# Row sums of the softmax in the first local attention: from a VectorE reduction to two mask columns in the product with V

## The chip, the cores and the metric

The kernel is one launch on one core of a Trainium2 chip. The metric is the device time of that core in microseconds (us), the median over several executions. The core's engines run their own instruction streams and meet only at semaphores: TensorE (PE; its weight loads are listed apart as PEld), VectorE (DVE), ScalarE (ACT), GpSimd (POOL), and SyncE (SP) for transfers. All of this kernel's matmuls are float32, and each one shows as two records in the trace.

## The reference

The program is a small language model tower of two layers over 64 x 256 tokens with 64 channels: embedding with a layer norm, a recurrent attention, a mixture of 8 experts, then windowed attention, then a graph attention that gates 4 experts. The change concerns the windowed attention alone ("first local attention", `L1_attn`):

```python
def _L1_attn_ref(x, qkv_w, qkv_b, proj_w, proj_b):
    H, W = (8, 64); HD = C // H                       # 8 heads of 8 channels, windows of 64 tokens
    qkv = (xw @ qkv_w + qkv_b).reshape(Bv, nW, W, 3, H, HD)
    q, k, v = (qkv[..., 0, :, :], qkv[..., 1, :, :], qkv[..., 2, :, :])
    attn = jnp.einsum('bwihd,bwjhd->bwhij', q, k) * HD ** (-0.5)
    attn = jax.nn.softmax(attn, axis=-1)
    out = jnp.einsum('bwhij,bwjhd->bwihd', attn, v).reshape(Bv, nW, W, Cv)
    return out @ proj_w + proj_b
...
h = h + _L1_attn_ref(_layernorm(h, axis=-1), ...)
```

There are 16384 tokens, so 256 windows of 64.

## The kernel before, in words

The 16384 tokens are 128 tiles of 128 rows (two windows of 64 tokens each). The attention takes four tiles at a time: four "lanes" (`AL`), each with its own two PSUM banks (`ps[0]` for small things, `ps[1]` for the 128 x 512 scores) and its own buffers, in a loop of `AI` = 32 iterations. The order is written out by hand. Each engine runs through a list of steps (`A_STEPS`), and each step is issued for lane 0, 1, 2, 3 before the next step begins (`step`). A step waits by `need` for the counters of the steps it depends on, and adds one to its lane's counter of its own engine.

The steps of one iteration, with the engine: `xs` (ACT, copy of the normalised tile), `xT` (PE, turn it), `xTs` (ACT), `qkv` (PE), `q` (ACT, two 64 x 64 copies, L817), `kb` (DVE, keys times the head mask, 128 x 512, L1193), `vb` (DVE, values times a two-column mask `vmask`, L1196), `sc` (PE, scores of 8 heads, 128 x 512), `mx` (DVE, row maxima, L1198), `sb` (DVE, scores less maxima into `B.E`, L1199), `ex` (ACT, exp of `B.E`, L819), `sm` (DVE, row sums of `B.E`, 128 x 512 to 128 x 8, L1200), `PT` (PE, turn the exponentials), `PTs` (ACT, copy to SBUF, L820), `rc` (DVE, reciprocal of the 8 sums, L1201), `pv` (PE, product with V: 8 matmuls per lane with 64 x 16 outputs, a pair of heads each), `on` (DVE, that product times the reciprocals, L1202), `oT` (PE, turn the result), `oTs` (ACT, L821), `pj` (PE, output projection), `h` (DVE, add to the residual, L1205).

The values in `B.V` are laid out by window and pair of heads. Of 128 rows (turned: a pair of heads by 64 keys), head 0 of the pair uses the first 64 and head 1 the last 64; `vmask` has a one in its column 0 for the former and in its column 1 for the latter. `xT` of the next iteration waits for `h` of its lane, so iterations hardly overlap. In some iterations VectorE also does a piece of an unrelated index preparation (`prepare`), in front of `kb`. Ahead of the loop VectorE makes the masks and clears or fills parts of the lanes' buffers (L1136 to L1143); the first `xT` of a lane waits for that. Every matmul is recorded at the helper line L389, so PE groups are told apart by their shapes.

Of the kernel before, what the change touches and what calls it, by code (L numbers as in the profile page):

```python
# [19 lines left out]
ACT_STEPS="h0s xs V th za sgt tw ta sq e1 e2 e3 lnk rn BKs Ats gts bons p2s p4s p8s EEs MKVs E2s Z0s W1Ts S1 S2 S3 Os osq lnv rstd yTs".split()  # L20
DVE_STEPS="oneh sg w cs cm a kq ssm kn A R b0 B t1 kp K rk g1 g2 l o d1 d2 d4 d8 Z1 W U1 U2 U3 mu oc var on gw gb bv ob og h".split()
COLS="b_w b_a k_k k_a r_k mr mw mk mv ma mg b_w2 b_a2 nk_a".split()
A_STEPS=dict(pe="xT qkv sc PT pv oT pj".split(), act="xs xTs q ex PTs oTs".split(), dve="kb vb mx sb sm rc on h".split())
G_STEPS=dict(pe="xT hg".split(), act="xs xTs hgs".split(), dve="ms rs md rd".split())
Y_STEPS=dict(pe=["h0","h1","y0","h2","y1","h3","y2","y3"], act=[f"g{e}" for e in range(4)], dve=["b0","b1"])
NE=262144; EC=NE//P
# [28 lines left out]
def prog(nc, x, embT_d, w1T_d, tb1_d, w2T_d, rows_d, proj_d, wv_d, ag_d, lora_d, bg_d, wo_d, cols_d,  # L55
         gam_d, wr_d, br_d, w1_d, b1_d, w2_d, b2_d, qkv_d, proj1_d, wg_d, att_d, lw1_d, lb1_d, lw2_d, lb2_d, fin_d, edges, out):
    with ExitStack() as ctx:
        sb=lambda n,s,d=F32: ctx.enter_context(nc.sbuf_tensor(n,s,d))
# [66 lines left out]
        for l in range(LANES):  # L125
            B=Lane(PS[4*l:4*l+4],sem(f"pe_step_{l}"),sem(f"act_step_{l}"),sem(f"dve_step_{l}"),1); L.append(B)
# [34 lines left out]
        iot=sb("iota8",[P,8]); iot_i=sb("iota8_i",[P,8],I32); mk_i=sb("mask_iota",[P,2],I32); mkf=sb("mask_iota_f",[P,2])  # L161
# [9 lines left out]
        take=bump(C0+8192,D0)  # L171
# [4 lines left out]
        for l in range(2):  # L176
            B=Lane(PS[4*l:4*l+4],None,None,None,0); FL.append(B)
# [4 lines left out]
        s_gw=sem("ffn0_gates"); s_wt=sem("ffn0_gates_turned"); s_ws=sem("ffn0_gates_copied"); s_fc=sem("ffn0_constants"); s_gs=sem("gate_rows_stored"); NK=NT//8  # L182
        AL=lanes("attn1",4,2,first=1); take=bump(C0+8192,D0)
        for B in AL:
            B.xs=take([D]); B.xT=take([P]); B.Q=take([P]); B.K=take([8,D]); B.V=take([2,D]); B.E=take([8,D])
            B.PT=take([4,P]); B.mx=take([8]); B.rs=take([8]); B.o=take([D]); B.oT=take([P])
        GL=lanes("gat",2,4,first=1); take=bump(C0+8192,D0)
        for B in GL:
# [199 lines left out]
        def _(pe):  # L388
            mm=lambda o,a,b,st=True,sp_=True: nc.tensor.matmul(o,a,b,start=st,stop=sp_,skip_group_check=True)  # L389
# [5 lines left out]
            for v in range(2):  # L395
                r=mm(ps0[1][:,v*D:(v+1)*D],hT[:,v*P:(v+1)*P],w2T[:,:])
# [242 lines left out]
            with pe.Fori(0,AI) as i:  # L639
                def step(fn,*names):  # L640
                    for B in AL:
                        need(pe,B,A_STEPS,i,*names)
                        fn(B).then_inc(B.pe,1)
                def xT(B):
                    pe.wait_ge(B.dve,i*len(A_STEPS["dve"])+1)
                    return mm(B.ps[0][0:D,0:P],B.xs,ident[:,:])
                step(xT,"act:xs")
                def qkv(B):
                    for h,s in HALVES:
                        w=slice(h*D,(h+1)*D)  # L650
                        mm(B.ps[0][s,P:P+D],aw[0:D+1,0:D],B.xT[0:D+1,w])
                        mm(B.ps[0][s,P+D:2*P],aw[0:D+1,D:2*D],B.xT[0:D+1,w])

                        for _,s2 in HALVES: r=mm(B.ps[0][s2,2*P+h*D:2*P+(h+1)*D],B.xT[0:D+1,w],aw[0:D+1,2*D:3*D])
                    return r
                step(qkv,"act:xTs")
                step(lambda B: mm(B.ps[1][:,:],B.Q,B.K.rearrange("p h j -> p (h j)")),"act:q","dve:kb")
                def PT(B):
                    for g in range(4): r=mm(B.ps[1][:,g*P:(g+1)*P],B.E[:,2*g:2*g+2,:].rearrange("p a b -> p (a b)"),ident[:,:])
                    return r  # L660
                step(PT,"act:ex","dve:sb")
                def pv(B):
                    for h,s in HALVES:
                        for g in range(4):
                            r=mm(B.ps[0][s,384+g*16:384+(g+1)*16],B.PT[:,g,h*D:(h+1)*D],B.V[:,h,g*16:(g+1)*16])
                    return r
                step(pv,"act:PTs","dve:vb")
                step(lambda B: mm(B.ps[0][0:D,0:P],B.o,ident[:,:]),"dve:on")
                step(lambda B: mm(B.ps[0][:,448:512],B.oT[0:D+1],ap[0:D+1]),"act:oTs")
            ended(pe,AL,A_STEPS,AI)  # L670

            with pe.Fori(0,GI) as i:
# [37 lines left out]
        def _(act):  # L710
# [162 lines left out]
        def _(dve):  # L873
            V=nc.vector; n=[0]
            def lk(ins):
                n[0]+=1; ins.then_inc(s_v,1); dve.wait_ge(s_v,n[0])
# [260 lines left out]
            lk(V.tensor_scalar(mk_i[:,0:1],mk_i[:,0:1],6,None,ALU.logical_shift_right))  # L1137
            lk(V.tensor_copy(mkf[:,:],mk_i[:,:]))
            V.tensor_scalar(hmask,iot[:,:],mkf[:,1:2],None,ALU.is_equal)
            V.tensor_scalar(vmask,iot[:,0:2],mkf[:,0:1],None,ALU.is_equal)  # L1140
            for B in AL:
                V.memset(B.xT[D:D+1],1.0); V.memset(B.oT[D:D+1],1.0)
                V.memset(B.Q[0:D,D:P],0.0); V.memset(B.Q[D:P,0:D],0.0).then_inc(B.dve,1)  # L1143
            for B in AL: dve.wait_ge(B.dve,1)
            dve.wait_ge(s_w2,16*8)
            h8=lambda t: t.unsqueeze(2).broadcast_to((P,8,D))
            sc=lambda B: B.ps[1][:,:].rearrange("p (h j) -> p h j",h=8)
# [39 lines left out]
            for i in range(AI):  # L1187
                prepare(i)
                def step(fn,*names):
                    for l,B in enumerate(AL):  # L1190
                        need(dve,B,A_STEPS,i,*names)
                        fn(B,l).then_inc(B.dve,1)
                step(lambda B,l:V.tensor_tensor(B.K,B.ps[0][:,P+D:2*P].unsqueeze(1).broadcast_to((P,8,D)),h8(hmask),ALU.mult),"act:q")  # L1193
                def vb(B,l):
                    v=lambda t: t.rearrange("p (g e d) -> p g e d",g=8,e=2)
                    return V.tensor_tensor(v(B.V.rearrange("p w f -> p (w f)")),v(B.ps[0][:,2*P:3*P]),vmask.unsqueeze(1).unsqueeze(3).broadcast_to((P,8,2,8)),ALU.mult)  # L1196
                step(vb,"pe:qkv")
                step(lambda B,l:V.tensor_reduce(B.mx,sc(B),AX.X,ALU.max),"pe:sc")  # L1198
                step(lambda B,l:V.tensor_tensor(B.E,sc(B),h8(B.mx),ALU.subtract),"dve:mx")  # L1199
                step(lambda B,l:V.tensor_reduce(B.rs,B.E,AX.X,ALU.add),"act:ex")  # L1200
                step(lambda B,l:V.reciprocal(B.rs,B.rs),"dve:sm")  # L1201
                step(lambda B,l:V.tensor_tensor(B.o.rearrange("p (h d) -> p h d",h=8),B.ps[0][:,384:448].rearrange("p (h d) -> p h d",h=8),B.rs.unsqueeze(2).broadcast_to((P,8,8)),ALU.mult),"pe:pv","dve:rc")  # L1202
                def hh(B,l):
                    v=H[:,bass.ds(i*4+l,1),:]
                    return V.tensor_tensor(v,v,B.ps[0][:,448:512].unsqueeze(1),ALU.add)  # L1205
                step(hh,"pe:pj")
            ended(dve,AL,A_STEPS,AI)
            norm(2)
# [87 lines left out]
            for g in range(NG):  # L1296
# [47 lines left out]
                for u in range(N//8):  # L1344
# [6 lines left out]
                    v=H[:,k*8:k*8+8,:]  # L1351
# [37 lines left out]
```

## Time and profile before

| | |
|---|---|
| median of 3 executions | 6361.67 us (6355.64 to 6379.33) |
| the profiled execution's own time | 6358.16 us |
| its span, first to last instruction | 6356.4 us |
| this attention in it (first `kb` to last `h`) | 2171 to 2757 us, 586 us |
| in that stretch: PE busy, DVE busy, ACT busy | 500.92, 423.27, 283.52 us |
| mean granted TensorE clock, whole span / this stretch | 0.653 / 0.94 |

Busy time is time in which an engine has an instruction under way; overlapping matmul records are counted once. In the timeline, "x4" means four instructions merged into one row, whose duration is from the first's start to the last's end; the bracket is the engine's idle time before the row and what ended it. A granted clock of 1.0 is 2.4 GHz, 0.5 is 1.2 GHz.

### The profile page before, as it was taken

How to read it: one execution, taken by the hardware profiler on the slowest of the kernel's cores; microseconds unless marked ns; L12 is line 12 of the kernel's file. 1: busy time of each engine (PE TensorE's matmuls, PEld its weight loads, DVE VectorE, ACT ScalarE, POOL GpSimd, SP SyncE). 2: the span in 40 equal slices, each digit the busy share in tenths (PEclk: the TensorE clock that was granted, in tenths of full speed). 3: DMA queues.
4: the chain of work that ended last, by engine and by line, in shares of the span. 5: the costliest groups of instructions: out<-in, count | busy, mean ns of one | idle time of the engine just before them, and what ended most of it. 6: DMA issues, size and time to landing. Idle time of an engine off the chain costs nothing. (4 is left out here: it accounts for less than half of the span.)

```text
span 6356.4 us, 72100 instructions
## 1 busy us (share of the span) xinstructions
PE 2622.9 (41%) x28363; PEld 1932.8 (30%) x28363; DVE 2338.0 (37%) x4995; ACT 1191.9 (19%) x2701; POOL 2664.5 (42%) x2593
## 2 busy tenths in 40 slices
PE   5776776765898688855234554400000000000000
PEld 4665665664422367744122332200000000000000
DVE  7754555557535676751011111311111111110136
ACT  3333333333333344431001110100000000000000
POOL 0000000000354400025755455477777777777753
PEclk9888888887778799975555555555555555555555
DMA  0022122211466240001111111111110111101113
GB/s 28 5 35 34 28 37 36 32 21 30 103 147 161 59 27 0 0 12 28 43 28 31 36 42 29 44 20 20 19 19 15 18 19 19 19 14 19 19 45 103
DMA packets 317184, 229.32 MB, mean 36 GB/s; under 512 B 178045, under 2 KB 264878, under 8 KB 314606
## 3 DMA queue, kind: packets, MB, share of 16 engines
q1 hardware_dynamic: 213582, 179.40, 13.2%
q0 software_dynamic: 82016, 33.49, 4.5%
q10 hardware_dynamic: 21344, 13.11, 0.8%
q8 instruction: 163, 2.67, 0.2%
q14 instruction: 79, 0.65, 0.0%
HBM read 153.09 MB, written 72.71 MB: 36 GB/s over the span
## 5 line engine op out<-in xcount | busy, mean ns | idle before, releaser
L389 PE MATMUL bank<-arena 64*64 64x64 f32 (+12 forms) x26246 | 2329.7, 287 | 1249.3 <-ACT arena L849 370.3
L377 POOL DMA_INDIRECT arena<-node_table,arena x2048 | 2118.8, 1035 | 918.0 <-issue 631.9
L389 PEld LDWEIGHTS bank<-arena 64*64 64x64 f32 (+5 forms) x26246 | 1661.7, 163 | 1903.2 <-issue 1035.0
L703 PE MATMUL bank<-ident,arena 128*20 128x128 f32 x3 | 0.8, 407 | 1996.1 <-remote 1996.1
L354 POOL MEMSET arena<- 128x512 f32 x1 | 0.5, 529 | 1521.1 <-DVE h_res L1042 1521.1
L703 PEld LDWEIGHTS bank<-ident,arena 128*20 128x20 f32 x3 | 0.3, 112 | 1996.4 <-remote 1996.3
L1243 DVE COPY arena<-arena 128x4 f32<-128x4 f32 x32 | 5.5, 170 | 1320.2 <-DMA arena<-node_table,arena 1319.8
L369 POOL DMA_INDIRECT edge_dst_terms<-arena,start_idx x128 | 125.8, 983 | 728.5 <-DVE arena L1218 688.6
L851 ACT ACTIVATE arena<-arena 128x512 f32<-128x512 f32 x32 | 20.1, 629 | 2017.8 <-issue 1334.4
L1231 DVE TENSOR_TENSOR arena<-bank,arena 128x512 f32<-128x512 f32 x64 | 43.6, 691 | 952.6 <-remote 845.3
L389 PE MATMUL bank<-ident,arena 128*128 128x128 f32 (+2 forms) x2048 | 301.0, 320 | 180.4 <-ACT arena L819 81.5
L389 PEld LDWEIGHTS bank<-ident,arena 128*128 128x128 f32 (+2 forms) x2048 | 268.9, 193 | 215.1 <-DVE arena L1199 107.8
L849 ACT ACTIVATE arena<-bank,arena 128x512 f32<-128x512 f32 x128 | 83.8, 687 | 908.2 <-remote 716.8
L1132 DVE TENSOR_TENSOR arena<-arena 128x512 f32<-128x512 f32 x256 | 170.3, 691 | 188.9 <-PE bank L389 108.0
L1258 DVE TENSOR_TENSOR_SCAN arena<-arena 128x64 f32<-128x64 f32 x640 | 197.1, 373 | 108.4 <-issue 107.3
L358 POOL DMA_INDIRECT arena<-row_pivots,pivot_row_idx x128 | 132.2, 1033 | 227.5 <-DVE pivot_row_idx L1104 109.4
L796 ACT ACTIVATE arena<-bank,arena 128x512 f32<-128x512 f32 x256 | 160.5, 689 | 271.8 <-PE bank L389 228.4
L363 POOL DMA_INDIRECT arena<-sorted_keys,key_block_idx x128 | 144.4, 1128 | 135.0 <-DVE arena L1132 76.9
L385 POOL DMA_INDIRECT arena<-sums_sorted,end_idx x128 | 134.6, 1052 | 40.3 <-issue 38.7
L949 DVE TENSOR_TENSOR arena<-arena 128x1024 f32<-128x1024 f32 x116 | 141.8, 1223 | 2.5
L950 DVE TENSOR_TENSOR arena<-arena 128x1024 f32<-128x1024 f32 x116 | 141.4, 1219 | 0.0
L819 ACT ACTIVATE arena<-arena 128x512 f32<-128x512 f32 x128 | 77.5, 630 | 162.0 <-DVE arena L1199 162.0
(352 smaller groups left out, 2653.3 us busy)
## 6 DMA issues: line engine op xcount, KB each, us to landing
arena<-gate_rows SPq DMA_DIRECT2D x256, 256.0 KB
arena<-node_table,arena POOLq DMA_INDIRECT x2048
sums_sorted<-arena SPq DMA_DIRECT2D x32, 768.0 KB
expert_out<-arena SPq DMA_DIRECT2D x64, 256.0 KB
arena<-expert_out SPq DMA_DIRECT2D x16, 1024.0 KB
sort_exchange<-arena SPq DMA_DIRECT2D x14, 1024.0 KB, 3.9
arena<-in_x_dram ACTq DMA_DIRECT2D x34, 256.0 KB, 3.3
edge_dst_terms<-arena SPq DMA_DIRECT2D x1, 4096.0 KB, 21.0
```

The lines of the kernel that those rows point to most:

```text
L358: G.indirect_dma_start(out=land2[:,t,:],out_offset=None,in_=piv_d,in_offset=bass.IndirectOffsetOnAxis(ap=idx1[:,t:t+1],axis=0)).then_inc(s ...
L363: G.indirect_dma_start(out=land3[:,t,:],out_offset=None,in_=keysb,in_offset=bass.IndirectOffsetOnAxis(ap=idx2[:,c*(NT//2)+t:c*(NT//2)+t+1] ...
L369: G.indirect_dma_start(out=ad_e,out_offset=bass.IndirectOffsetOnAxis(ap=sidx[:,t:t+1],axis=0), in_=nodeG[:,t,20:24],in_offset=None,bounds_ ...
L377: G.indirect_dma_start(out=rch[:,j%NB,c,:],out_offset=None,in_=tbl, in_offset=bass.IndirectOffsetOnAxis(ap=gidx[:,j*CW+c:j*CW+c+1],axis=0) ...
L385: G.indirect_dma_start(out=ends[:,t,:],out_offset=None,in_=sums_d,in_offset=bass.IndirectOffsetOnAxis(ap=eidx[:,t:t+1],axis=0)).then_inc(s ...
L389: mm=lambda o,a,b,st=True,sp_=True: nc.tensor.matmul(o,a,b,start=st,stop=sp_,skip_group_check=True)
L796: A.activation(B.hT[:,n%3,:],B.ps[n%3][:,:],ACT.Gelu,bias=fb1[:,n%8:n%8+1]).then_inc(B.ge,1)
L849: A.activation(B.hT[:,u%2,:],B.ps[u%2][:,:],ACT.Gelu,bias=lb1[:,u:u+1]).then_inc(B.act,1)
L949: V.tensor_tensor(y[:,:,0,:],x[:,:,0,:],x[:,:,1,:],ALU.min)
L950: lk(V.tensor_tensor(y[:,:,1,:],x[:,:,0,:],x[:,:,1,:],ALU.max))
L1132: V.tensor_tensor(B.hS[:,x%2,:],B.hT[:,x%3,:],GB[:,l,x%3,:],ALU.mult).then_inc(B.mu,1)
L1258: last=V.tensor_tensor_scan(R[:,:,f],xe[:,0,:,head(f)],R[:,:,f],carry[:,1-b,f:f+1],ALU.mult,ALU.add)
```

## The change

The row sums of the exponentials are no longer reduced on VectorE. Each pair of heads in `B.V` gets two more columns that hold `vmask`, written once ahead of the loop; the product `pv` then has 64 x 18 outputs, of which the last two are the two heads' row sums. The step `sm` is gone. The reciprocal reads the sums in PSUM and waits for `pv`; the product with the reciprocals reads 16 of every 18 columns. As the product now takes 72 columns, the output projection goes to columns 128 to 191 of the same bank.

```diff
-A_STEPS=dict(... dve="kb vb mx sb sm rc on h".split())
+A_STEPS=dict(... dve="kb vb mx sb rc on h".split())
-            B.xs=take([D]); ... B.V=take([2,D]); B.E=take([8,D])
+            B.xs=take([D]); ... B.V=take([2,4,18]); B.E=take([8,D])
 def pv(B):
-                            r=mm(B.ps[0][s,384+g*16:384+(g+1)*16],B.PT[:,g,h*D:(h+1)*D],B.V[:,h,g*16:(g+1)*16])
+                            r=mm(B.ps[0][s,384+g*18:384+(g+1)*18],B.PT[:,g,h*D:(h+1)*D],B.V[:,h,g,:])
-                step(lambda B: mm(B.ps[0][:,448:512],B.oT[0:D+1],ap[0:D+1]),"act:oTs")
+                step(lambda B: mm(B.ps[0][:,P:P+D],B.oT[0:D+1],ap[0:D+1]),"act:oTs")
-            V.tensor_scalar(vmask,iot[:,0:2],mkf[:,0:1],None,ALU.is_equal)
+            lk(V.tensor_scalar(vmask,iot[:,0:2],mkf[:,0:1],None,ALU.is_equal))
             for B in AL:
                 V.memset(B.xT[D:D+1],1.0); V.memset(B.oT[D:D+1],1.0)
+                V.tensor_copy(B.V.rearrange("p w g f -> p (w g) f")[:,:,16:18],vmask.unsqueeze(1).broadcast_to((P,8,2)))
 def vb(B,l):
-                    v=lambda t: t.rearrange("p (g e d) -> p g e d",g=8,e=2)
-                    return V.tensor_tensor(v(B.V.rearrange("p w f -> p (w f)")),v(B.ps[0][:,2*P:3*P]),vmask...,ALU.mult)
+                    v=B.V.rearrange("p w g f -> p (w g) f")[:,:,0:16].rearrange("p g (e d) -> p g e d",e=2)
+                    return V.tensor_tensor(v,B.ps[0][:,2*P:3*P].rearrange(...),vmask...,ALU.mult)
-                step(lambda B,l:V.tensor_reduce(B.rs,B.E,AX.X,ALU.add),"act:ex")
-                step(lambda B,l:V.reciprocal(B.rs,B.rs),"dve:sm")
-                step(lambda B,l:V.tensor_tensor(B.o...,B.ps[0][:,384:448]...,B.rs...,ALU.mult),"pe:pv","dve:rc")
+                pairs=lambda B: B.ps[0][:,384:456].rearrange("p (g f) -> p g f",f=18)
+                step(lambda B,l:V.reciprocal(B.rs.rearrange("p (g e) -> p g e",e=2),pairs(B)[:,:,16:18]),"pe:pv")
+                step(lambda B,l:V.tensor_tensor(B.o...,pairs(B)[:,:,0:16]...,B.rs...,ALU.mult),"dve:rc")
-                    return V.tensor_tensor(v,v,B.ps[0][:,448:512].unsqueeze(1),ALU.add)
+                    return V.tensor_tensor(v,v,B.ps[0][:,P:P+D].unsqueeze(1),ALU.add)
```

On VectorE, from the sums to the products with the reciprocals, an iteration of the kernel before has these rows in order (L1200 `sm`, L1201 `rc`, L1202 `on`; `attn1_pe_2` is the TensorE counter of lane 2, `attn1_dve_2` VectorE's own):

```order
L1200 TENSOR_REDUCE arena<-arena 128x8 [waits attn1_act_3]
L1201 RECIPROCAL arena<-arena 128x8 [waits attn1_dve_0]
L1201 RECIPROCAL arena<-arena 128x8 [waits attn1_dve_1]
L1201 RECIPROCAL arena<-arena 128x8 [waits attn1_dve_2]
L1201 RECIPROCAL arena<-arena 128x8 [waits attn1_dve_3]
L1202 TENSOR_TENSOR arena<-bank,arena 128x64 [waits attn1_dve_0,attn1_pe_0]
L1202 TENSOR_TENSOR arena<-bank,arena 128x64 [waits attn1_dve_1,attn1_pe_1]
L1202 TENSOR_TENSOR arena<-bank,arena 128x64 [waits attn1_dve_2,attn1_pe_2]
L1202 TENSOR_TENSOR arena<-bank,arena 128x64 [waits attn1_dve_3,attn1_pe_3]
```

At the same place the changed kernel has these (L1200 is now `sb`, L1202 `rc`, L1203 `on`):

```order
L1200 TENSOR_TENSOR arena<-bank,arena 128x512 [waits attn1_dve_3]
L1202 RECIPROCAL arena<-bank 128x8 [waits attn1_pe_0]
L1202 RECIPROCAL arena<-bank 128x8 [waits attn1_pe_1]
L1202 RECIPROCAL arena<-bank 128x8 [waits attn1_pe_2]
L1202 RECIPROCAL arena<-bank 128x8 [waits attn1_pe_3]
L1203 TENSOR_TENSOR arena<-bank,arena 128x64 [waits attn1_dve_0]
L1203 TENSOR_TENSOR arena<-bank,arena 128x64 [waits attn1_dve_1]
L1203 TENSOR_TENSOR arena<-bank,arena 128x64 [waits attn1_dve_2]
L1203 TENSOR_TENSOR arena<-bank,arena 128x64 [waits attn1_dve_3]
```

The four waits for TensorE have moved from the products to the reciprocals, and the first lane's product now stands behind the last lane's reciprocal in VectorE's queue.

On TensorE the order of the product, the turning of the result and the projection is unchanged. The changed kernel, from the last lane's product on:

```order
L389 MATMUL bank<-arena 64x18 [waits attn1_dve_3,attn1_act_3]
L389 MATMUL bank<-arena 64x18 x7
L200 REGISTER_ALU
L389 MATMUL bank<-ident,arena 64x128 [waits attn1_dve_0]
L389 MATMUL bank<-ident,arena 64x128 [waits attn1_dve_1]
L389 MATMUL bank<-ident,arena 64x128 [waits attn1_dve_2]
L389 MATMUL bank<-ident,arena 64x128 [waits attn1_dve_3]
L200 REGISTER_ALU
L389 MATMUL bank<-arena 128x64 [waits attn1_act_0]
```

The outputs are two columns wider; `oT` (64 x 128) still waits, lane by lane, for VectorE's `on`.

## Rows read from the trace of the kernel before

**Rows 1.** The page: span, and section 1, busy time of each engine.

```profile
span 6356.4 us, 72100 instructions
...
PE 2622.9 (41%) x28363; PEld 1932.8 (30%) x28363; DVE 2338.0 (37%) x4995; ACT 1191.9 (19%) x2701; POOL 2664.5 (42%) x2593
```

**Rows 2.** Window of this attention: length; PE, PEld, DVE, ACT, POOL; PEclk, DMA, GB/s.

```profile
2171.00:2757.00 586.00, 500.92 (x6108) 410.95 (x6105) 423.27 (x1061) 283.52 (x886) 0.00 (x0) 0.94 0.13 8
```

**Rows 3.** Waits in the same stretch: waiter <- awaited, total, times, longest (us).

```profile
ACT arena L819 <- DVE arena L1199: 162.0, 32, 6.1
...
DVE arena L1202 <- PE bank L389: 90.6, 128, 2.6
...
DVE arena L1193 <- ACT arena L817: 43.5, 29, 2.5
```

**Rows 4.** Groups of instructions by form, same stretch: busy, mean ns | idle before, releaser.

```profile
L389 PE MATMUL bank<-arena 128*64 128x16 f32 x2048 | 78.7, 212 | 0.0
...
L1200 DVE TENSOR_REDUCE arena<-arena 128x8 f32<-128x512 f32 x128 | 78.6, 678 | 0.0
...
L389 PE MATMUL bank<-ident,arena 128*64 128x128 f32 x504 | 70.0, 281 | 0.4 <-DVE arena L1202 0.2
...
L1202 DVE TENSOR_TENSOR arena<-bank,arena 128x64 f32<-128x64 f32 x128 | 28.8, 225 | 90.6 <-PE bank L389 90.6
...
L1201 DVE RECIPROCAL arena<-arena 128x8 f32<-128x8 f32 x128 | 12.8, 165 | 0.0
```

**Rows 5.** Timeline, end of one iteration, all engines: start, duration, instruction, [idle before].

```profile
2491.38 2.45 DVE L1200 TENSOR_REDUCE arena<-arena 128x8 f32<-128x512 f32 x4
...
2493.74 0.40 DVE L1201 RECIPROCAL arena<-arena 128x8 f32<-128x8 f32 x4
...
2495.67 2.19 PEld L389 LDWEIGHTS bank<-arena 128*64 128x64 f32 x61
...
2496.61 0.23 DVE L1202 TENSOR_TENSOR arena<-bank,arena 128x64 f32<-128x64 f32 x1 [2.46 <-PE bank L389]
...
2497.75 0.32 PE L389 MATMUL bank<-ident,arena 128*64 128x128 f32 x1
...
2498.02 0.86 PE L389 MATMUL bank<-ident,arena 128*64 128x128 f32 x6
...
2498.17 0.22 DVE L1202 TENSOR_TENSOR arena<-bank,arena 128x64 f32<-128x64 f32 x1 [0.29 <-PE bank L389]
...
2498.22 0.95 ACT L821 COPY arena<-bank 64x128 f32<-64x128 f32 x4 [1.86 <-PE bank L389]
...
2498.81 1.10 PE L389 MATMUL bank<-arena 65*128 65x64 f32 x8
...
2499.28 0.89 DVE L1205 TENSOR_TENSOR h_res<-h_res,bank 128x64 f32<-128x64 f32 x4 [0.89 <-PE bank L389]
...
2499.84 0.85 PEld L389 LDWEIGHTS bank<-ident,arena 128*64 128x64 f32 x8
```

**Rows 6.** Timeline of VectorE: the first product of an iteration with reciprocals, L1202.

```profile
2185.01 0.23 DVE L1202 TENSOR_TENSOR arena<-bank,arena 128x64 f32<-128x64 f32 x1 [1.01 <-PE bank L389]
...
2202.22 0.23 DVE L1202 TENSOR_TENSOR arena<-bank,arena 128x64 f32<-128x64 f32 x1 [1.01 <-PE bank L389]
...
2515.45 0.23 DVE L1202 TENSOR_TENSOR arena<-bank,arena 128x64 f32<-128x64 f32 x1 [2.64 <-PE bank L389]
...
2735.27 0.22 DVE L1202 TENSOR_TENSOR arena<-bank,arena 128x64 f32<-128x64 f32 x1 [1.02 <-PE bank L389]
```

**Rows 7.** Windows while the turned weights are multiplied, in two iterations.

```profile
2490.40:2493.20 2.80, 2.74 (x13) 2.75 (x14) 2.80 (x6) 2.31 (x4) 0.00 (x0) 0.50 0.00 0
...
2547.90:2551.00 3.10, 3.10 (x39) 2.98 (x38) 2.43 (x8) 2.56 (x5) 0.00 (x0) 1.00 0.00 0
```

**Rows 8.** Timeline, preparation ahead of the first iteration.

```profile
2166.77 0.29 PEld L389 LDWEIGHTS bank<-ident,arena 128*64 128x64 f32 x2 [38.36 <-DVE arena L1143]
```

**Rows 9.** Group over the whole span: a VectorE operation that reads SBUF alone.

```profile
L1217 DVE TENSOR_TENSOR arena<-arena 128x64 f32<-128x64 f32 x64 | 13.8, 223 | 186.3 <-ACT arena L836 140.3 <-issue 46.0
```

More of the change, by code:

```diff
@@ L22 @@
 COLS="b_w b_a k_k k_a r_k mr mw mk mv ma mg b_w2 b_a2 nk_a".split()
-A_STEPS=dict(pe="xT qkv sc PT pv oT pj".split(), act="xs xTs q ex PTs oTs".split(), dve="kb vb mx sb sm rc on h".split())
+A_STEPS=dict(pe="xT qkv sc PT pv oT pj".split(), act="xs xTs q ex PTs oTs".split(), dve="kb vb mx sb rc on h".split())
 G_STEPS=dict(pe="xT hg".split(), act="xs xTs hgs".split(), dve="ms rs md rd".split())
@@ L184, in prog @@
         for B in AL:
-            B.xs=take([D]); B.xT=take([P]); B.Q=take([P]); B.K=take([8,D]); B.V=take([2,D]); B.E=take([8,D])
+            B.xs=take([D]); B.xT=take([P]); B.Q=take([P]); B.K=take([8,D]); B.V=take([2,4,18]); B.E=take([8,D])
             B.PT=take([4,P]); B.mx=take([8]); B.rs=take([8]); B.o=take([D]); B.oT=take([P])
@@ L1194, in vb @@
                 def vb(B,l):
-                    v=lambda t: t.rearrange("p (g e d) -> p g e d",g=8,e=2)
-                    return V.tensor_tensor(v(B.V.rearrange("p w f -> p (w f)")),v(B.ps[0][:,2*P:3*P]),vmask.unsqueeze(1).unsqueeze(3).broadcast_to((P,8,2,8)),ALU.mult)
+                    v=B.V.rearrange("p w g f -> p (w g) f")[:,:,0:16].rearrange("p g (e d) -> p g e d",e=2)
+                    return V.tensor_tensor(v,B.ps[0][:,2*P:3*P].rearrange("p (g e d) -> p g e d",g=8,e=2),vmask.unsqueeze(1).unsqueeze(3).broadcast_to((P,8,2,8)),ALU.mult)
                 step(vb,"pe:qkv")
@@ L1199, in _ @@
                 step(lambda B,l:V.tensor_tensor(B.E,sc(B),h8(B.mx),ALU.subtract),"dve:mx")
-                step(lambda B,l:V.tensor_reduce(B.rs,B.E,AX.X,ALU.add),"act:ex")
-                step(lambda B,l:V.reciprocal(B.rs,B.rs),"dve:sm")
-                step(lambda B,l:V.tensor_tensor(B.o.rearrange("p (h d) -> p h d",h=8),B.ps[0][:,384:448].rearrange("p (h d) -> p h d",h=8),B.rs.unsqueeze(2).broadcast_to((P,8,8)),ALU.mult),"pe:pv","dve:rc")
+                pairs=lambda B: B.ps[0][:,384:456].rearrange("p (g f) -> p g f",f=18)
+                step(lambda B,l:V.reciprocal(B.rs.rearrange("p (g e) -> p g e",e=2),pairs(B)[:,:,16:18]),"pe:pv")
+                step(lambda B,l:V.tensor_tensor(B.o.rearrange("p (g e d) -> p g e d",g=4,e=2),pairs(B)[:,:,0:16].rearrange("p g (e d) -> p g e d",e=2),B.rs.rearrange("p (g e) -> p g e",e=2).unsqueeze(3).broadcast_to((P,4,2,8)),ALU.mult),"dve:rc")
                 def hh(B,l):
                     v=H[:,bass.ds(i*4+l,1),:]
-                    return V.tensor_tensor(v,v,B.ps[0][:,448:512].unsqueeze(1),ALU.add)
+                    return V.tensor_tensor(v,v,B.ps[0][:,P:P+D].unsqueeze(1),ALU.add)
                 step(hh,"pe:pj")
```

## The prediction

> **What bounds the kernel now.** I read four views, in this order. The page first: over the span no engine is above 42% [rows 1], so the shares of the whole run decide nothing, and the question is what ends the waits in the one stage that is changed. The window of that stage comes next: 586 us, PE busy for 500.92 of them, VectorE for 423.27, ScalarE for 283.52 [rows 2]. No engine is full; what repeats 32 times is a chain that passes from engine to engine, and each engine waits somewhere on it. Third, the waits: ScalarE waits 162.0 us for `sb` before `ex`, VectorE waits 90.6 us for TensorE before `on`, and 43.5 us for ScalarE before `kb` [rows 3]. So the chain runs on VectorE from `kb` to `sb`, and from the exponentials to the end of the iteration on TensorE and ScalarE. Fourth, the timeline of one iteration's end [rows 5] shows where `sm` lies. It starts at 2491.38 and ends at 2493.83, the four reciprocals are done at 2494.14, and VectorE then stands idle for 2.46 us until the product with V is there at 2496.61. The idle time before `sm` and `rc` is 0.0 in all 128 cases and nothing shows them on a path [rows 4]; the wait behind them is never under 1.01 us [rows 6].
>
> **What is removed.** 128 reductions of 678 ns, 78.6 us of VectorE time [rows 4]. The cover that hides them is TensorE and ScalarE turning the exponentials, copying them and multiplying by V. With `sm` gone nothing on that path starts earlier: `PT` needs `ex` and `sb`, `pv` needs the copy. What is late next is the same wait for `pv`, which grows from 1.01 or some 2.5 us by about 2.45. Gain on the path: 0.
>
> **What is moved.** The reciprocals now wait for `pv`, and because each step runs over all four lanes, `on` of lane 0 stands behind `rc` of lane 3. Before, `on` of lane l started as soon as its product was there: 2496.61 for lane 0, 2498.17 for lane 3, 0.52 us apart, and so the turning `oT` of lane 0 was issued at 2497.75, right behind TensorE's last product matmuls [rows 5]. After, in the same iteration:
> - the last product is seen at 2498.17, and `rc` of lane 3 starts then (the other three fit between the products);
> - `on` of lane 0 follows. Four reciprocals in a row take 0.40 us at 0.165 each [rows 4, 5], which makes a start every (0.40 - 0.165)/3 = 0.08 us. So it starts at 2498.25 and ends at 2498.25 + 0.23 = 2498.48;
> - TensorE starts `oT` some 0.05 us later, at 2498.53. (I take 0.05 for one engine's answer to another: in [rows 5] ScalarE's copy starts at 2498.22, 0.47 after the turning begins, and the two records of a turning, 0.11 apart with the last 0.32 long, take 0.43 of that.)
> - 2498.53 against 2497.75 is 0.78 us later.
>
> The other three products need not stretch this. Eight records of `oT` go at 0.107 us each (six take 0.86 with the last some 0.32 long), so a lane needs 0.21, and `on` has a start every 0.15 or so, by the same difference of start and duration as the reciprocals. Nothing behind it absorbs the delay. `pj` begins at 2498.81, where the last record of `oT` ends, the additions wait 0.89 us for `pj`, the next iteration's `xT` is issued at 2499.84 on `pj`'s heels [rows 5], and `kb` waits for ScalarE again, 29 times in the stage [rows 3]. In the iterations where VectorE does index work first, that work starts after the last addition, which is as late. So the whole 0.78 comes back in each iteration: I take 0.77, times 32 = 24.6 us.
>
> Bounds of this unknown step. From below: only VectorE's part counts, if TensorE catches up: `on` of lane 3 starts 0.08 + 3 x 0.145 = 0.52 us later, 16.6 us. From above: the reciprocal does not overlap the product behind it (0.165) and takes the time of a whole product, since it reads PSUM with a stride: 0.23 + 0.23 + 0.05 = 0.51 after 2498.17, 0.93 in all, 29.8 us. I stay near the nearest row, four reciprocals in a row.
>
> The Trainium skill speaks against the nearest row here: "VectorE: DVE Perf Modes", section on the TRN2 errata, prices a VectorE instruction at 58 cycles plus its elements from SBUF and 120 from PSUM; by that the moved reciprocal would be an estimated 65 ns dearer, some 2 us over 32 iterations. This trace doesn't agree: 64 elements with a PSUM input take 225 ns [rows 4], and 223 ns from SBUF alone [rows 9]. I keep the row.
>
> **What is added.** Two more columns in each product matmul. The 16-column loads stand 2.19/61 = 0.036 us apart [rows 5], the 128-column turnings 0.107; the line between them gives 0.0006 us a column, 64 records x 2 columns x 0.0006 = 0.08 us an iteration, 2.6 us at most. From below it is 0, if the weight loads, which stand without a gap over those 2.19 us, set the distance. I take 0, the nearer row. Ahead of the loop, one waited mask and four small copies of 16 elements: the first `xT` already waits for these VectorE steps, 38.36 us of idle ending at 2166.77 [rows 8], so they lie on the path; five small instructions between 0.08 and 0.165 each come to 0.4 to 0.8 us, I take 0.7. `vb` writes as many elements as before: 0. `pj`'s other columns: 0.
>
> **TensorE's clock** is the second term. In 13 iterations the first `on` waits 1.01 or 1.02 us, in 19 it waits 2.42 to 2.65 [rows 6], which shows the first two, a long one, and the last but one. Iterations without index work are then 17.21 us long (2202.22 less 2185.01) or 18.84 (2515.45 less 2496.61 of [rows 5]). The windows say why: with the turned weights under multiplication the granted clock was 0.50 (1.2 GHz) in one such iteration and 1.00 (2.4 GHz) in another [rows 7], and ahead of that stretch the exponentials, and TensorE with them, had waited for VectorE's `sb` [rows 3]. So a fall costs 1.45 to 1.63 us, in 19 of 32 iterations 30 us. That wait isn't changed, and the number of falls I leave at 19; but since otherwise equal iterations differ, a longer iteration can shift it by some 6 either way, 10 us.
>
> **Sum.** 24.6 + 0.7 + 0 = 25.3 us. On the profiled execution's own time, 6358.16 (its span and 1.8 us around it), that gives 6383.5; the median of the runs lies 3.5 us above that execution, so for a median I say 6385, 0.4% slower. About 0.5%, 32 us, is what a measurement of this kernel can tell from no change.
>
> **The rivals.**
> - *The new wait costs clock too (slower).* TensorE now stands still for 0.8 us between `pv` and `oT`, behind a stretch of small matmuls. If the clock falls there, or the longer iteration makes it fall in all 32 iterations, the 13 that are spared now cost 1.55 each, 20 us: 25 + 20 = 45, 6406. It decides from 5 further falls on. For it: the falls come next to a wait for VectorE [rows 6, 7]. Against: the present ones come at a wait of over 2 us. 20%. In the Trainium skill, "TensorE: Matmul & The Clock Gate", section on loop structure, says a VectorE copy out of PSUM between groups does not break the warmth; by it this rival would be out, but this trace has 19 falls around VectorE's steps.
> - *The delay is smaller.* VectorE's 0.52 us alone counts, or some falls go away with the new period: 16.6 - 9 = 8 us, 6370. For it: the first four iterations in a row have no fall. 12%.
> - *VectorE's relief is worth its time (faster).* If `sm` were on the path, 78.6 us would go: 6283. Against: the wait of at least 1.01 us behind it in all 32 iterations. 3%.
>
> **How the numbers follow.** The forecast has 65%. Within 0.5% are the forecast and the smaller delay, 77%; slower is the first rival with the edge of the forecast, 20%; faster is the third, 3%. The forecast's own range is 6372 to 6396. For 8 in 10 the low end takes in the smaller delay less its spared falls, 6364, and the high end the upper bound with all falls: 6361.7 + 29.8 + 2.6 + 0.8 + 15 = 6410.
>
> **What would show it.** Right: no reduction behind `exp`; VectorE's long wait now before the reciprocal, some 3.5 or 5 us long; the four `on` in one row of about 0.67 us; `oT` starting 0.78 us later against the first product; iterations of 18.0 or 19.6 us. Wrong: `oT` starts before the last reciprocal; iterations of 17.2; more or fewer than 19 iterations at a granted clock of 0.50; or reciprocals of more than 0.2 us.

## The result, and the profile after

| | before | after |
|---|---|---|
| median | 6364.71 us (6355.64 to 6379.33, 4 runs) | 6395.29 us (6389.11 to 6405.97, 4 runs) |
| ratio | | 1.0048, 95% interval 1.0024 to 1.0071 |
| profiled execution's own time | 6358.16 us | 6389.11 us |

A later measurement, with 12 runs of the change (e5 below), gave 1.0017 (1.0001 to 1.0032). Both say slower; the two intervals share 1.0024 to 1.0032, 15 to 20 us, and the iterations, read below, show 23 to 24.

The page's first lines after, against [rows 1]: VectorE has lost 71.6 us of busy time, and the span is 31.0 us longer.

```profile
span 6387.4 us, 71848 instructions
...
PE 2628.2 (41%) x28363; PEld 1940.6 (30%) x28363; DVE 2266.4 (35%) x4871; ACT 1190.0 (19%) x2701; POOL 2663.8 (42%) x2593
```

The waits in the attention after (waiter <- awaited: total, times, longest), against [rows 3]:

```profile
DVE arena L1202 <- PE bank L389: 178.8, 128, 6.4
ACT arena L819 <- DVE arena L1200: 162.8, 32, 7.2
...
DVE arena L1194 <- ACT arena L817: 42.0, 28, 2.0
...
PEld bank L389 <- DVE arena L1203: 15.6, 32, 0.5
```

The wait for `sb` is what it was (162.0 before). VectorE's wait for TensorE has doubled, from 90.6 to 178.8 us: the 78.6 us of reduction and the reciprocals' time have become idle time. The last row is new, 15.6 us in 32 pieces: TensorE now waits for VectorE's `on` in every iteration.

The groups by form (busy, mean ns | idle before), against [rows 4]:

```profile
L389 PE MATMUL bank<-arena 128*64 128x18 f32 x2048 | 78.7, 214 | 0.0
...
L389 PE MATMUL bank<-ident,arena 128*64 128x128 f32 x504 | 68.5, 279 | 12.5 <-DVE arena L1203 12.5
...
L1202 DVE RECIPROCAL arena<-bank 128x8 f32<-128x8 f32 x128 | 26.6, 207 | 178.8 <-PE bank L389 178.8
...
L1203 DVE TENSOR_TENSOR arena<-bank,arena 128x64 f32<-128x64 f32 x128 | 18.1, 203 | 0.0
```

The 18-column product costs what the 16-column one did (78.7 us of both), the turning waits 12.5 us for `on` where it had waited 0.2, and the reciprocals are apart now: 207 ns each, where four in a row had a mean of 165.

The timeline of one iteration's end and the start of the next one's wait (start, duration, instruction [idle before]), against [rows 5]:

```profile
2484.93 3.83 PE L389 MATMUL bank<-ident,arena 128*128 128x128 f32 x32 [2.52 <-ACT arena L819]
...
2488.69 2.36 PEld L389 LDWEIGHTS bank<-arena 128*64 128x64 f32 x64
...
2489.63 0.21 DVE L1202 RECIPROCAL arena<-bank 128x8 f32<-128x8 f32 x1 [3.70 <-PE bank L389]
...
2491.19 0.21 DVE L1202 RECIPROCAL arena<-bank 128x8 f32<-128x8 f32 x1 [0.31 <-PE bank L389]
2491.31 0.56 DVE L1203 TENSOR_TENSOR arena<-bank,arena 128x64 f32<-128x64 f32 x4
2491.54 0.85 PEld L389 LDWEIGHTS bank<-ident,arena 128*64 128x64 f32 x8 [0.49 <-DVE arena L1203]
...
2492.01 0.91 ACT L821 COPY arena<-bank 64x128 f32<-64x128 f32 x4 [2.63 <-PE bank L389]
2492.55 0.97 PEld L389 LDWEIGHTS bank<-arena 65*128 65x128 f32 x8 [0.17 <-issue]
...
2493.03 0.89 DVE L1206 TENSOR_TENSOR h_res<-h_res,bank 128x64 f32<-128x64 f32 x4 [1.15 <-PE bank L389]
2493.59 0.85 PEld L389 LDWEIGHTS bank<-ident,arena 128*64 128x64 f32 x8
...
2509.20 0.21 DVE L1202 RECIPROCAL arena<-bank 128x8 f32<-128x8 f32 x1 [5.33 <-PE bank L389]
```

The last lane's product is seen at 2491.19. Its reciprocal starts there; `on` of lane 0 starts 0.12 us later at 2491.31, and the turning `oT` another 0.23 later, at 2491.54. So `oT` starts 0.35 us behind that moment; before, it started 0.42 us ahead of it (2497.75 against 2498.17), 0.77 us in all. `pj` follows 1.36 us behind it (0.64 before), the additions 1.84 (1.11), the next `xT` 2.40 (1.67): 0.72 to 0.73 us later each. Of the 0.77, 0.04 are won back: the eight records of `oT` now run without the last product matmuls between them. From 2489.63 to 2509.20 is an iteration of 19.57 us, against 18.84 in [rows 5, 6]; the short ones are 17.94 against 17.21.

The windows after (length; PE, PEld, DVE, ACT, POOL; PEclk, DMA share, GB/s): the whole attention, the turning of the exponentials in the iteration above, the new wait with what surrounds it, and the turning in the next iteration:

```profile
2165.89:2777.11 611.22, 514.18 (x6107) 421.92 (x6104) 350.20 (x932) 282.03 (x886) 0.00 (x0) 0.94 0.13 7
2484.90:2488.50 3.60, 3.58 (x32) 3.58 (x32) 1.03 (x2) 3.35 (x6) 0.00 (x0) 1.00 0.00 0
2488.70:2493.50 4.80, 4.41 (x81) 4.14 (x80) 1.78 (x11) 1.99 (x9) 0.00 (x0) 1.00 0.00 0
2504.60:2508.20 3.60, 3.60 (x20) 3.54 (x19) 0.00 (x0) 1.71 (x3) 0.00 (x0) 0.58 0.00 0
```

The attention took 611.22 us; from the first `kb` to the last `h` it was 585.1 before. The granted clock fell to 0.5 in parts of the same place as before, the turning of the exponentials (mean 0.58 in the last window, 1.00 in the iteration above), in 18 iterations after and 19 before. Around the new wait it is 1.00.

### The profile page after: what moved, and what is told of

Same layout as the page of the kernel before. It is cut to its first block, busy times and chain, and to the rows that moved or that the text cites. A ratio compares the mean times of both kernels' runs of the same rounds, so it can differ in the third digit from the quotient of the medians.

```text
span 6387.4 us, 71848 instructions
## 1 busy us (share of the span) xinstructions
PE 2628.2 (41%) x28363; PEld 1940.6 (30%) x28363; DVE 2266.4 (35%) x4871; ACT 1190.0 (19%) x2701; POOL 2663.8 (42%) x2593
## 4 chain that ended last, share of the span: by engine, by line
PE 30%; issue 24%; DVE 14%; another core or an unknown queue 13%; POOL 12%; ACT 4%; DMA 1%; ACTq 0%; SPq 0%; DVEq 0%; POOLq 0%
PE bank L389 30%; POOL arena L377 12%; DVE arena L1194 1%; DVE arena L1199 1%; ACT arena L849 1%; DMA arena<-gate_rows 1%; DVE arena L1348 1%; DVE arena L949 1%; DVE arena L950 1%; DVE arena L1058 0%; DVE ln_stat L1057 0%; DVE arena L1197 0%; DVE arena L1064 0%; ACT arena L819 0%
```

## The experiments

Each ran between 6 and 12 times beside the kernel before on the same chip, and is compared with those runs only: the kernel before had medians of 6328.96 us beside e1 to e4, 6351.88 beside e5 to e8 and 5865.20 beside e9 and e10. Why the third is some 460 us faster is not known. Most of it lies behind the attention, where no run changes an instruction (from the last `h` to the end 3159 us in e9, 3573 in e4). Beside the ratio stand two readings of the profile that are finer than it: the length of an iteration between two equal instructions, without and with a fall of the clock, and the number of iterations with one.

**e1_no_sum.** The reduction alone is taken away; the reciprocals work on a buffer of ones, so the division by the row sums is left out.

```diff
-                step(lambda B,l:V.tensor_reduce(B.rs,B.E,AX.X,ALU.add),"act:ex")
-                step(lambda B,l:V.reciprocal(B.rs,B.rs),"dve:sm")
+                step(lambda B,l:V.reciprocal(B.rs,B.rs),"act:ex")
```

> The kernel before without the row sums: VectorE's reduction is left out, the reciprocals work on a buffer set to 1 once, so the division by the row sums is left out. Theory 1 (the cost of the change is the order of VectorE's steps; the reduction was hidden): iterations stay at 17.21 and 18.84 us, the first product waits about 2.5 us longer, and the time stays that of the kernel before within 10 us. Rival 1 (VectorE's time is worth its length): 2.45 us less in each of 32 iterations, 78 us faster. Rival 2 (the clock term follows VectorE's load): the number of iterations with the granted clock at 0.50 moves away from 19 by 6 or more.

Measured: 6320.69 us against 6328.96, ratio 0.9999 (0.9977 to 1.0020). Iterations of 17.21 and 18.85 us; the first `on` waits 2.80 instead of 1.01 us. 15 iterations with a fall. The reduction was hidden; 78.6 us of VectorE time are worth nothing here that this measurement, good to 0.2%, could see.

**e2_late_reciprocal.** One wait is added to the kernel before.

```diff
-                step(lambda B,l:V.reciprocal(B.rs,B.rs),"dve:sm")
+                step(lambda B,l:V.reciprocal(B.rs,B.rs),"dve:sm","pe:pv")
```

> The kernel before, with its reduction and its 16-column products, but each reciprocal also waits for its lane's product with V. Nothing else is changed. Theory 1 (order): the first product with reciprocals stands behind the last lane's reciprocal; iterations of 17.21 + 0.7 = 17.9 and 19.5 us, 20 to 25 us slower than before, like the change. The reciprocal reads SBUF, so its start distance of 0.08 us and length of 0.165 should make the delay a little smaller than the change's 0.73, 0.65 to 0.7. Rival (the width of the product, or the PSUM read, costs the time): 17.21 as before, 0 us.

Measured: 6355.62 us against 6328.96, ratio 1.0034 (1.0014 to 1.0054). Iterations of 17.94 and 19.57 us, to the hundredth those of the change, with the reduction in place and products of 16 columns. The groups (busy, mean ns | idle before):

```profile
L1201 DVE RECIPROCAL arena<-arena 128x8 f32<-128x8 f32 x128 | 26.0, 203 | 105.2 <-PE bank L389 105.2
...
L1202 DVE TENSOR_TENSOR arena<-bank,arena 128x64 f32<-128x64 f32 x128 | 18.7, 207 | 0.4 <-issue 0.4
```

So the order of the steps is the whole of the 0.73 us. The expected 0.65 to 0.7 for a reciprocal that reads SBUF was wrong: standing apart it takes 203 ns from SBUF and 207 from PSUM.

**e3_wide_product_alone.** The kernel before with the mask columns, their preparation, the projection's new columns and 18-column products of the change; the sums are unread.

```diff
-            ... B.V=take([2,D]) ...
+            ... B.V=take([2,4,18]) ...
-                            r=mm(B.ps[0][s,384+g*16:384+(g+1)*16],...,B.V[:,h,g*16:(g+1)*16])
+                            r=mm(B.ps[0][s,384+g*18:384+(g+1)*18],...,B.V[:,h,g,:])
```

> The kernel before plus the two mask columns in V and 18-column products, whose sums nobody reads; reduction and reciprocals stay where they were. Theory 1 (order): only the preparation, 0.7 us once; iterations of 17.21 us. Rival (width): two columns in 64 records an iteration, 0.08 us by the line between the 16- and the 128-column form, 2.6 us in all; if the width were the change's cost, 0.73 us an iteration and 23 us.

Measured: 6335.02 us against 6328.96, ratio 1.0008 (0.9988 to 1.0027). Iterations of 17.21 and 18.84 us, 16 of them with a fall. Its timeline (first and last `on` of one iteration, then the wide product and first `on` of the next):

```profile
2417.23 0.23 DVE L1204 TENSOR_TENSOR arena<-bank,arena 128x64 f32<-128x64 f32 x1 [2.48 <-PE bank L389]
...
2418.79 0.23 DVE L1204 TENSOR_TENSOR arena<-bank,arena 128x64 f32<-128x64 f32 x1 [0.29 <-PE bank L389]
...
2435.14 2.29 PE L389 MATMUL bank<-arena 128*64 128x18 f32 x61
...
2436.07 0.23 DVE L1204 TENSOR_TENSOR arena<-bank,arena 128x64 f32<-128x64 f32 x1 [2.64 <-PE bank L389]
```

The four products are seen 1.56 us apart from first to last, as before. Two columns cost nothing.

**e4_lane_by_lane.** The change, with reciprocal and product of a lane issued together.

```diff
-                step(lambda B,l:V.reciprocal(...,pairs(B)[:,:,16:18]),"pe:pv")
-                step(lambda B,l:V.tensor_tensor(B.o...,ALU.mult),"dve:rc")
+                for l,B in enumerate(AL):
+                    need(dve,B,A_STEPS,i,"pe:pv")
+                    V.reciprocal(...,pairs(B)[:,:,16:18]).then_inc(B.dve,1)
+                    need(dve,B,A_STEPS,i,"dve:rc")
+                    V.tensor_tensor(B.o...,ALU.mult).then_inc(B.dve,1)
```

> The change, but VectorE issues reciprocal and product of lane 0, then of lane 1, and so on. Theory 1 (order): the turning of lane 0 starts right behind the last product with V again; what is left is that the last lane's product ends some 0.25 us later than before (a reciprocal of 0.21 and its own wait), so at most 0.25 an iteration: 17.2 to 17.5 us, 0 to 8 us slower than the kernel before and 15 to 23 faster than the change. Rival (the PSUM read or the width costs the time, or the clock does): iterations stay at 17.9 us and the time at about 25 us over the kernel before.

Measured: 6326.68 us against 6328.96, ratio 0.9991 (0.9975 to 1.0006). Iterations of 17.45 and 19.08 us. Its timeline:

```profile
2494.60 0.21 DVE L1204 RECIPROCAL arena<-bank 128x8 f32<-128x8 f32 x1 [3.70 <-PE bank L389]
2494.84 0.23 DVE L1206 TENSOR_TENSOR arena<-bank,arena 128x64 f32<-128x64 f32 x1
2495.12 0.21 DVE L1204 RECIPROCAL arena<-bank 128x8 f32<-128x8 f32 x1
...
2495.74 0.32 PE L389 MATMUL bank<-ident,arena 128*64 128x128 f32 x1
...
2496.16 0.21 DVE L1204 RECIPROCAL arena<-bank 128x8 f32<-128x8 f32 x1
...
2496.41 0.22 DVE L1206 TENSOR_TENSOR arena<-bank,arena 128x64 f32<-128x64 f32 x1
2496.68 0.19 PEld L389 LDWEIGHTS bank<-ident,arena 128*64 128x64 f32 x2 [0.31 <-DVE arena L1206]
...
2497.05 1.10 PE L389 MATMUL bank<-arena 65*128 65x64 f32 x8
```

`oT` of lane 0 starts at 2495.74, 0.42 us ahead of the last product seen (2496.16), as in the kernel before. What stays is the last lane: its reciprocal and product end at 2496.63, and the last turning waits 0.31 us for them (2496.68). That is the 0.24 us over 17.21, 8 us in all. The time is below that, and the profile shows a likely reason: only 9 iterations had a fall, where e1 and e3, beside the same runs, had 15 and 16 and the profile of before 19. At 1.63 us each that is 10 to 16 us less. It isn't this one execution alone: the mean granted clock over the span is 0.658 in the 12 executions of e4 and 0.655 in the 35 of the kernel before. No run tests it further.

**e5_change_again.** The changed kernel once more.

> The changed kernel once more, on the same chip and beside the same runs of the kernel before as the three below. Theory 1 (order, 0.73 us an iteration, 23.4 in all, and 0.7 of preparation): 24 us slower than before, ratio 1.0038. Rival (something outside this attention adds to it, as the first measurement's 31 us hint): 31 us, ratio 1.0048.

Measured: 6366.60 us (12 runs) against 6351.88, ratio 1.0017 (1.0001 to 1.0032), so about 11 us, less than either theory said: both missed. But the iterations are again 17.94 and 19.56 us, 17 of them with a fall. The interval takes in 20 us at its end and not 24. So the total of a whole run tells less than its interval suggests, and what the order costs is read from the iterations and from e9 and e10.

**e6_filled_wait.** The kernel of e4 with unused matmuls in TensorE's wait for `sb`.

```diff
                 step(lambda B: mm(B.ps[1][:,:],B.Q,B.K...),"act:q","dve:kb")
+                for B in AL:
+                    need(pe,B,A_STEPS,i,"dve:vb")
+                    for _ in range(2): mm(B.ps[0][:,456:512],B.Q,B.K.rearrange("p h j -> p (h j)")[:,0:56])
```

> The change with VectorE lane by lane, and two unused matmuls a lane (56 columns into free columns of the bank) on TensorE behind the scores, while it would wait for VectorE; they cost nothing on the path if they end before the turning of the exponentials may start. Theory on the clock (the granted clock falls to 0.50 because TensorE stands still in that wait): no or few iterations with a fall, nearly all of 17.45 us, 15 to 30 us faster than the same kernel without them, so about 15 to 25 below the kernel before. Rival (the falls have another cause): 10 to 20 iterations still fall, iterations of 17.45 and 19.1 us as without them, the time of the kernel before.

Measured: 6336.02 us against 6351.88, ratio 0.9970 (0.9950 to 0.9990). All iterations without index work or a transfer beside them are 17.45 us, and one alone shows the long wait of a fall. Timeline and window:

```profile
2484.90 7.55 PE L389 MATMUL bank<-arena 65*64 65x64 f32 x88
...
2493.25 3.83 PE L389 MATMUL bank<-ident,arena 128*128 128x128 f32 x32 [0.79 <-ACT arena L822]
```

```profile
2178.00:2736.00 558.00, 528.32 (x6496) 439.17 (x6493) 357.52 (x915) 276.32 (x875) 0.00 (x0) 0.98 0.13 8
```

TensorE's wait before the turning is 0.79 us where it had been 2.52, and the mean clock of the stretch is 0.98. The window leaves out the last 11 us; over the whole attention TensorE is busy for 538.14 us of 569.01, where e4 has 491.81 of 578.10. More work on TensorE, and less time: with that wait filled the falls of the clock are gone but for one. The whole run is 0.3% faster than the kernel before; against e4 (ratio 0.9991) the intervals overlap, and e9 below is the clearer test.

**e7_scores_lane_by_lane.** The kernel of e4, and row maximum and subtraction lane by lane too, with `vb` behind them.

```diff
-                step(vb,"pe:qkv")
-                step(lambda B,l:V.tensor_reduce(B.mx,sc(B),AX.X,ALU.max),"pe:sc")
-                step(lambda B,l:V.tensor_tensor(B.E,sc(B),h8(B.mx),ALU.subtract),"dve:mx")
+                for l,B in enumerate(AL):
+                    need(dve,B,A_STEPS,i,"pe:sc")
+                    V.tensor_reduce(B.mx,sc(B),AX.X,ALU.max).then_inc(B.dve,1)
+                    need(dve,B,A_STEPS,i,"dve:mx")
+                    V.tensor_tensor(B.E,sc(B),h8(B.mx),ALU.subtract).then_inc(B.dve,1)
+                step(vb,"pe:qkv")
```

> The change with reciprocal and product lane by lane, and also row maximum and subtraction lane by lane, with the values' mask (vb) behind them. Theory 1 (the chain runs through VectorE from kb to sb and then through the turning): the first exponential starts about 2.5 us earlier, the last about 0.5, and the turning of the last lane no longer queues behind the others; 1.4 us less an iteration than 17.45, about 16.1, so 35 to 40 us faster than before, and more if the shorter wait of TensorE spares falls of the clock (up to 30 us more). Rival (TensorE's own work bounds the iteration from the turning on): under 0.5 us an iteration, 16 us.

Measured: 6288.51 us against 6351.88, ratio 0.9900 (0.9880 to 0.9919), faster. Iterations of 16.21 us, 1.24 less than in e4, none with a fall. The first reciprocal of two iterations:

```profile
2483.42 0.21 DVE L1207 RECIPROCAL arena<-bank 128x8 f32<-128x8 f32 x1 [1.96 <-PE bank L389]
...
2499.64 0.21 DVE L1207 RECIPROCAL arena<-bank 128x8 f32<-128x8 f32 x1 [1.96 <-PE bank L389]
```

**e8_scores_lane_by_lane_with_sums.** The same edit on the kernel before: reduction on VectorE, 16 columns, reciprocals ahead of `pv`.

> The kernel before, with its reduction on VectorE, and with row maximum and subtraction lane by lane and vb behind them. Theory 1: the path gets as short as in the run just before this one, and now the reduction is about to show: reductions and reciprocals end 3.65 us behind the last subtraction, the first product with V is there 2.6 us behind it and the last 4.2, so 0 to 0.2 us an iteration more than in the pure path; about 16.2 us, 35 to 40 us faster than before, the same within 8 us as with the sums on TensorE. Rival (VectorE's relief pays once the path is shorter): the reduction's 2.45 us come on top, iterations over 17.2 us and no gain.

Measured: 6282.04 us (6264.02 to 6302.42) against 6351.88, ratio 0.9891 (0.9871 to 0.9911): the fastest kernel of the study. An iteration is 15.96 us (the last `on` at 2486.01 and again at 2501.97), 0.25 less than with the sums on TensorE and less than the 16.2 expected; and the expected 35 to 40 us counted the path alone, without the falls. Its timeline, and the window of the attention:

```profile
2492.31 0.68 DVE L1199 TENSOR_REDUCE arena<-bank 128x8 f32<-128x512 f32 x1
...
2493.02 0.69 DVE L1201 TENSOR_TENSOR arena<-bank,arena 128x512 f32<-128x512 f32 x1
...
2493.75 0.63 ACT L819 ACTIVATE arena<-arena 128x512 f32<-128x512 f32 x1 [2.47 <-DVE arena L1201]
...
2494.50 0.97 PEld L389 LDWEIGHTS bank<-ident,arena 128*128 128x128 f32 x8 [0.88 <-DVE arena L1201]
...
2498.38 2.46 DVE L1203 TENSOR_REDUCE arena<-arena 128x8 f32<-128x512 f32 x4
...
2500.76 0.39 DVE L1204 RECIPROCAL arena<-arena 128x8 f32<-128x8 f32 x4
2501.07 0.61 DVE L1205 TENSOR_TENSOR arena<-bank,arena 128x64 f32<-128x64 f32 x3
...
2501.97 0.23 DVE L1205 TENSOR_TENSOR arena<-bank,arena 128x64 f32<-128x64 f32 x1 [0.30 <-PE bank L389]
```

```profile
2165.30:2681.40 516.10, 496.22 (x6107) 388.53 (x6104) 428.25 (x1061) 278.51 (x886) 0.00 (x0) 0.99 0.15 9
```

The turning starts at 2494.50, behind the first lane's subtraction instead of behind all maxima. Now VectorE has no slack left: the reductions start at 2498.38 right behind `vb`, reciprocals at 2500.76, the first `on` at 2501.07, and none of the first three waits. Yet it is in time, because the last `on` still waits 0.30 us for TensorE. The clock is 0.99 over the stretch. The order is worth 1.25 x 32 = 40 us and the clock 19 falls of 1.45 to 1.63 us, 30 us; 70 together. The attention went from 585.1 to 515.4 us between the two profiles, and the medians differ by 69.8. That the medians agree so closely is partly luck, since the falls are those of one execution.

**e9_before_filled** and **e10_change_filled.** The two unused matmuls a lane of e6 put into the kernel before and into the change, to have the change without the clock's part.

> The kernel before with the two unused matmuls a lane behind the scores, and nothing else. If the clock's falls come from TensorE's wait, they go here too: nearly all iterations of 17.21 us, and 14 to 19 falls of some 1.6 us spared, 20 to 30 us faster than the kernel before. Otherwise 0.

> The change with the same two unused matmuls. With no falls left in either kernel, this run against the one before it is the change without the clock's part. Theory 1 (order alone): iterations of 17.94 against 17.21, 0.73 x 32 = 23.4 us and 0.7 of preparation, 24 us between the two. Rival A (part of the change's cost is a larger number of falls): also 24, but the change alone against the kernel before shows more than these two. Rival B (there is a cost outside this attention): over 30 us between the two.

Measured: 5841.58 us and 5863.90 us (12 runs each), with 5865.20 for the kernel before beside them; ratios 0.9961 (0.9943 to 0.9980) and 1.0000 (0.9982 to 1.0018). The difference is 22.3 us. The window of e9 and the timeline of e10:

```profile
2130.00:2680.00 550.00, 521.53 (x6573) 440.92 (x6572) 416.80 (x1046) 280.63 (x880) 0.00 (x0) 1.00 0.14 8
```

```profile
2413.61 0.21 DVE L1205 RECIPROCAL arena<-bank 128x8 f32<-128x8 f32 x1 [3.70 <-PE bank L389]
...
2415.18 0.21 DVE L1205 RECIPROCAL arena<-bank 128x8 f32<-128x8 f32 x1 [0.31 <-PE bank L389]
2415.30 0.56 DVE L1206 TENSOR_TENSOR arena<-bank,arena 128x64 f32<-128x64 f32 x4
...
2431.55 0.21 DVE L1205 RECIPROCAL arena<-bank 128x8 f32<-128x8 f32 x1 [3.70 <-PE bank L389]
```

The mean clock of e9 in that window is 1.00, and TensorE's wait before the turning is 0.79 us in both. Iterations are 17.21 us in e9 and 17.94 in e10; e9 has one fall and e10 none. The first `on` of e9 and the first reciprocal of e10 stand 539.92 and 560.08 us apart over 31 iterations; 31 x 0.73 less the one fall that e9 had (1.63) and less 0.82 for an iteration beside a transfer, which took 1.58 longer in e9 and 0.76 in e10, is 20.2, as measured. Rival A asks for more in the change alone than in this pair; alone it showed 31 and 11 us, on either side of 22.3, so nothing ties part of the cost to a larger number of falls. Rival B asks for over 30 us; it isn't borne out, though each ratio is known only to 0.18%, 11 us. The two profiled spans differ by 25.1 us (5840.2 and 5865.3), of which some 4 lie ahead of the attention.

## Why the prediction was right, step by step

The path was right and so was its size, 24.6 us forecast and 23.4 measured for the moved wait. The total is less secure: the first measurement's median, 6395.29, lies 0.7 us inside the forecast's range of 6372 to 6396, and the second says 11 us where the first says 31. That the first fell inside at all is partly luck, since some 5 of the 31 us between the profiled executions come from outside the attention.

- *What is removed: 0.* Right. e1 takes the reduction away and the iterations keep their 17.21 us. The wait behind it grew, as the waits after show.
- *What is moved: 0.77 us, times 32 = 24.6.* The mechanism was right, and e2 shows it alone. The sum of its three parts, 0.08 to the first product, 0.23 for it and 0.05 to TensorE, was 0.36 and measured 0.35, but not by its parts: the reciprocal stands 0.12 ahead of the product, and the product with its answer takes 0.23 together. What was too large is the step from `oT`'s start to `pj`'s: of 0.77 us 0.73 arrive, since the turnings no longer share TensorE with the last products. 0.73 x 32 = 23.4.
- *What is added: 0 for the columns, 0.7 for the preparation.* The columns are right (e3). From the mask instruction to the first `kb` it is 5.72 us after (2160.17 to 2165.89), and it was 5.25 (2165.80 to 2171.05): 0.47.
- *The clock: 19 falls kept.* 18 after. They cost 18 x 1.63 = 29.3 us; before, 11 of 1.63 and 8 of 1.45, 29.5. No difference, in this pair of executions; over the runs without filled waits the number went from 9 to 19 (e7 and e8, with another path and no falls, apart). I had said that the number can move by some 6; e4's 9 is beyond that.
- *The dearer PSUM read.* By the Trainium skill's "VectorE: DVE Perf Modes", section on the TRN2 errata, an estimated 65 ns for the moved reciprocal. Two kernels whose reciprocals stand at the same place, each behind a wait, gave 203 ns (SBUF, e2) and 207 (PSUM, after), and iterations of the same length. The row was the better guide.
- *The sum.* Forecast 25.3 us; measured 31 and 11 in two measurements, 22.3 with the clock's falls taken out of both kernels, 23.4 + 0.5 by the iterations. (The median forecast has a slip: 25.3 us on 6361.67 is 6387, not 6385.) Of the 31.0 us between the two profiled spans some 26 lie in the attention: 23.4 for the order, 2.0 for the iteration beside a transfer (22.82 against 20.14 us, 0.73 of it the order's), and 1.1 in the first iteration, where VectorE's row maxima wait 1.01 and 1.01 us for the second and third lane's scores and 0.76 and 0.17 before. In both profiles the granted clock is 0.50 as these scores begin; it is 1.00 from 7 us behind the first `kb` after, and from 5 us behind it before. The other 4.9 are 5.2 us less ahead of the attention, in spite of the 0.5 added there, and some 10 more behind it, where no instruction was changed. That is within what equal code shows: in the profiles of e1 to e4 the first `kb` starts at 2146.23 to 2172.31 us, and from the last `h` to the end it takes 3572 to 3598 us. So chance suffices for it, though no run was made for it.
- *The rivals.* The new wait costs no clock: 1.00 in its window, no further falls. The smaller delay is out at 17.94 us. VectorE's relief is out by e1, and again by e8, where even the shortened path keeps the reduction hidden.
- *The signs.* The wait before the first reciprocal is 3.70 or 5.33 us, `oT` is 0.77 us later against the first product, the iterations 17.94 and 19.57 us: as forecast, and the four `on` take 0.56 us, not 0.67. Two signs that I had called wrong came true: 18 falls and not 19, and reciprocals of 207 ns, over 0.2 us. Neither speaks against the path. They were set too tight: the number of falls differs by four between e1 and before, whose short iterations are equal, and e2 has 203 ns for reciprocals that read SBUF, with the same iterations.

## What to carry to other kernels

When an engine's work is taken away, look at the wait right behind it: if it is there in every iteration, the work was hidden, and what decides is whether the replacement joins the path. In a schedule that runs each step over all lanes, an instruction that waits for the last lane stands in front of the first lane's next step; pair dependent steps lane by lane, and the engine behind can start at once. Here the better order of VectorE's steps (e8) gained three times what the change cost, 40 us by the shorter iteration and 30 by the falls that went with it, with no new operation.

## What I had not expected of the hardware

- A wait of 2.5 us on TensorE, in an iteration of 17, can cost more than itself: the granted clock falls in some of the iterations and the matmuls behind take 1.45 to 1.63 us longer. Eight unused matmuls an iteration in that wait left one such iteration of 32 (e6, e9) or none (e10), and gained 0.4% of the whole time on the kernel before. The wait is not all that decides: in the profile of before it is the same 2.52 us in iterations with a fall and in iterations without one. What picks them no run shows.
- How many iterations have a fall may depend on the length of the iteration: 15 to 19 at 17.21 us (before, e1, e3), 17 to 19 at 17.94 (after, e2, e5), where short and long mostly alternate, and 9 at 17.45 (e4), each number from one profiled execution. So two kernels that differ by 0.24 us an iteration can differ by 10 to 16 us for this alone.
- In one iteration a 4 MB store runs beside the attention. The transfers of the profile after in that stretch list it so (size, and time from issue to landing):

```profile
edge_dst_terms<-arena SPq DMA_DIRECT2D x1, 4096.0 KB, 20.7
```

The iteration beside it took 20.14 us in the profile of before, 22.82 after, 24.36 in e1, 26.90 in e2, 17.42 in e3 and 18.70 in e10: 0.2 to 7 us more than an iteration of its kernel without index work, with or without a fall as the case is. It moves the total by up to some microseconds whatever the kernel. That the store is the cause is not shown, since no run leaves it out.
